# Folding the lift of the softmax exponent into the rows of the maxima

## The reference

```python
q, k, v = (split_heads(ln(x) @ W.T) for W in (Wq, Wk, Wv))   # 4 x 16 heads, 1024 x 64
sim = einsum('bhid,bhjd->bhij', q, k) * DIM_HEAD ** -0.5
m = max(sim, axis=-1)
e = exp(sim - m)
attn = e / (sum(e, axis=-1) + 1e-10)
x = x + (attn @ v) @ Wo.T + bo
gate, y = fp4_linear(ln(x), w_gate), fp4_linear(ln(x), w_up)
x = x + fp4_linear(silu(gate) * y, w_down)
```

## Time and profile before

| | us |
|---|---|
| median of 3 runs | 1754.72 |
| the profiled execution | 1756.87 |
| its span in the trace | 1755.0 |
| PE busy | 1539.2 (88%) |
| DVE busy | 1435.4 (82%) |
| POOL busy | 1242.6 (71%) |
| ACT busy | 1218.8 (69%) |

### The profile page before, as it was taken

How to read it: one execution, slowest core, us unless ns; L and a number is a source line. 1 busy time by engine, 2 the same in 40 slices (tenths; PEclk the granted TensorE clock), 3 DMA queues, 4 the chain that set the end, 5 groups by cost and what they waited for, 6 DMA issues and landing times.

```text
span 1755.0 us, 35325 instructions
## 1 busy us (share of the span) xinstructions
PE 1539.2 (88%) x13828; PEld 1041.4 (59%) x13828; DVE 1435.4 (82%) x2441; ACT 1218.8 (69%) x2222; POOL 1242.6 (71%) x1369
## 2 busy tenths in 40 slices
PE   4798899999889988898988898888898888898966
PEld 2465566666666656565656665655665656666654
DVE  7778877777788888888888888888888888888767
ACT  3587778888667776677777677767676776677633
POOL 3587778888677777677776777767777777777753
PEclk7899999999999999999999999999999999999987
DMA  4000000000000000000000000000000000000000
GB/s 122 13 13 13 7 14 14 13 14 14 7 15 15 13 15 9 9 15 15 14 15 9 9 15 15 13 9 15 9 15 15 13 9 9 15 15 13 3 4 12
DMA packets 26372, 26.20 MB, mean 15 GB/s; under 512 B 4768, under 2 KB 18016, under 8 KB 26208
## 3 DMA queue, kind: packets, MB, share of 16 engines
q1 hardware_dynamic: 26208, 23.95, 5.7%
HBM read 4.80 MB, written 2.10 MB: 4 GB/s over the span
## 4 chain that ended last, share of the span: by engine, by line
DVE 43%; PE 40%; ACT 10%; POOL 4%; issue 3%; DMA 0%; DVEq 0%; ACTq 0%; POOLq 0%
DVE negm L818 13%; PE ob L548 11%; PE sm L502 7%; PE st L522 6%; PE st L520 6%; ACT probs L635 5%; DVE q_hl L766 4%; ACT k_hh L599 3%; DVE qv L982 3%; DVE qv L970 3%; DVE k_l L772 3%; DVE qv L980 3%; POOL p_low L386 2%; PE mb L463 2%; DVE q_small L966 2%
## 5 line engine op out<-in xcount | busy, mean ns | idle before, releaser
L386 POOL TENSOR_TENSOR p_low<-probs 128x512 f16<-128x512 f32 x1024 | 1086.9, 1072 | 403.8 <-ACT probs L635 402.5
L635 ACT ACTIVATE probs<-st,lift,exp_scale 128x512 f32<-128x512 f32 x1024 | 792.8, 778 | 302.2 <-PE st L522 278.3
L818 DVE TENSOR_REDUCE negm<-sm 128x1 f32<-128x1024 f32 x512 | 624.4, 1220 | 126.6 <-PE sm L502 121.2
L502 PE MATMUL sm<-k_hh,q_hl 128*128 128x512 f16 x1024 | 314.8, 390 | 122.6 <-DVE negm L818 119.7
L522 PE MATMUL st<-q_hm,k_l 66*128 66x512 f16 x1024 | 396.6, 387 | 0.0
L520 PE MATMUL st<-q_hl,k_hh 128*128 128x512 f16 x1024 | 394.5, 385 | 0.6 <-ACT probs L635 0.6
L548 PEld LDWEIGHTS ob<-v,probs 128*128 128x128 bf16 x4096 | 283.4, 99 | 128.3 <-issue 11.5
L548 PEld LDWEIGHTS ob<-v,p_low 128*128 128x128 f16 x4096 | 278.9, 98 | 124.9 <-issue 2.7
L548 PE MATMUL ob<-v,probs 128*128 128x129 f16 x4096 | 325.1, 222 | 0.1
L548 PE MATMUL ob<-v,p_low 128*128 128x129 f16 x4096 | 320.8, 221 | 2.0 <-POOL p_low L386 2.0
L649 ACT ACTIVATE oscl<-ob,rden 128x128 f32<-128x128 f32 x512 | 158.6, 364 | 53.9 <-DVE rden L808 53.8
(11 more groups left out here) (157 smaller groups left out, 1616.1 us busy)
## 6 DMA issues: line engine op xcount, KB each, us to landing
k_hh<-k_hh SPq DMA_DIRECT2D x64, 128.0 KB, 2.3
q_hm<-q_hl SPq DMA_DIRECT2D x64, 128.0 KB, 2.3
x<-x SPq DMA_DIRECT2D x4, 512.0 KB, 7.2
q_hm<-m_high SPq DMA_DIRECT2D x128, 1.0 KB
q_hm<-m_low SPq DMA_DIRECT2D x128, 1.0 KB
out<-x SPq DMA_DIRECT2D x24, 64.0 KB, 1.5
probs<-wq SPq DMA_DIRECT2D x1, 512.0 KB, 5.7
probs<-wk SPq DMA_DIRECT2D x1, 512.0 KB, 6.9
```

The costliest lines, as they stand in the source:

```text
L386: return pool.tensor_tensor(p_low[b][:, j, :], p, p.bitcast(BF16)[:, 1::2], ALU.subtract)
L502: pe.matmul(sm[:, s % 2, :], q_hl[n][:, t * P:(t + 1) * P], k_hh[n][:, (s % 2) * 512:(s % 2 + 1) * 512], start=True, stop=True).then_inc(s ...
L635: nc.scalar.activation(probs[k % 2][:, s, :], st[s % 2][:, :], ACT.Exp, bias=lift[:, 0:1], scale=exp_scale[:, head, pair:pair + 1]).then_i ...
L818: nc.vector.tensor_reduce(negm[k % 2][:, s // 2:s // 2 + 1], sm[:, :, :].rearrange("p a n -> p (a n)"), AX.X, ALU.max, negate=True).then_i ...
```

## The change

The lift is no longer added by the exponential, which now has no bias operand. It is added to the rows of the maxima: for each head the tile `lift` holds 64/1024 divided by the head's top scale (at most 2**14), so that the scale of the exponential turns it into 8 again. The job `m` therefore multiplies `negm` by a diagonal of 1/1024 with a matmul in place of the transpose, ACT adds the head's lift with the function Identity and a bias operand, and DVE adds it as a scalar operand. Where the cap of 2**14 holds, the lift is smaller, so the constant beside the sums is made for each head too: `eps_lifted` comes from the setup through one exponential, one more small DVE operation follows at the start of round 1, and L805 takes it as a scalar operand. The setup makes `ident_unit` on POOL and has three more DVE operations and one more activation.

```diff
--- before.py
+++ after.py
@@ -35,7 +35,7 @@
 LIFT = 64.0
 MAX_UNIT = 1024.0
 TINY = 2.0 ** -126
-EPS_LIFTED = SM_EPS * math.exp(SCALE * LIFT)
+LIFT_TOP = 2.0 ** 14
 VC = 2 * DH + 1
 OT = 256
 
@@ -164,7 +164,9 @@
         exp_scale = sb("exp_scale", [P, 2, PAIRS])
         k_inv = sb("k_inv", [P, PAIRS])
         k_scale = sb("k_scale", [P, PAIRS])
-        lift = sb("lift", [P, 1])
+        lift = sb("lift", [P, 2, PAIRS])
+        eps_lifted = sb("eps_lifted", [P, 2, PAIRS])
+        ident_unit = sb("ident_unit", [P, P])
         w_inv = sb("w_inv", [P, 3, PAIRS])
         wT = [sb(f"wT_{part}", [P, 3, PAIRS, P], F16) for part in ("high", "low")]
         wo_s = sb("wo_s", [P, PAIRS, DIM])
@@ -200,6 +202,7 @@
         s_ws = [sem(f"{w}_scaled") for w in ("wq", "wk", "wv", "wo")]
         s_ks = sem("head_scale_step")
         s_kt = sem("head_scale_turned")
+        s_le = sem("eps_lifted_made")
         s_wt = sem("w_turned")
         s_wh = sem("wT_high_made")
         s_we = sem("wT_low_made")
@@ -236,6 +239,11 @@
         ffn = Ffn(nc, sb, sem, st, sm_banks, ob, mb, probs, p_low, xn,
                   (stats, mv, var_eps, rstd), (eps, half))
 
+        def lift_of(g, unit):
+
+            pair = (g - 1 + unit // 4) % PAIRS
+            return lift[0:IT, unit // 2 % 2, pair:pair + 1]
+
         def output_of(g, q, k, bank):
 
             back = 1 if bank == 0 else 2
@@ -333,6 +341,10 @@
             pool.wait_ge(s_id, 1)
             pool.affine_select(out=ident[:, :], in_=ident[:, :], compare_op=ALU.not_equal, fill=1.0,
                                base=0, pattern=[[-1, P]], channel_multiplier=1).then_inc(s_id, 1)
+            pool.memset(ident_unit[:, :], 0.0).then_inc(s_id, 1)
+            pool.wait_ge(s_id, 3)
+            pool.affine_select(out=ident_unit[:, :], in_=ident_unit[:, :], compare_op=ALU.not_equal, fill=1.0 / MAX_UNIT,
+                               base=0, pattern=[[-1, P]], channel_multiplier=1).then_inc(s_id, 1)
             ffn.constants(pool)
             pool.wait_ge(s_hf, 2)
 
@@ -473,14 +485,15 @@
 
                     unit = JOBS[n][ON_PE][0]
                     wait(pe, s_mx, 4 * (4 * (g - 1) + unit + 2))
-                    last = pe.transpose(bank[0:IT, 0:P], negm[(unit + 1) % 2][:, :], ident[:, :])
+                    last = pe.matmul(bank[0:IT, 0:P], negm[(unit + 1) % 2][:, :], ident_unit[:, :], start=True, stop=True)
                 last.then_inc(mb_ready[JOBS[n][1]], 1)
 
             def round_(g, r, q):
                 prev, cur, nxt, ffn_x, ffn_h = flags(r)
                 if r == 1:
 
-                    pe.wait_ge(s_init, 8)
+                    pe.wait_ge(s_init, 7)
+                    pe.wait_ge(s_id, 4)
                     pe.wait_ge(s_ws[3], 1)
                 for k in range(4):
                     head, half = k // 2, k % 2
@@ -582,6 +595,9 @@
                 nc.scalar.activation(wT[0][:, n // 2, n % 2 * 4:n % 2 * 4 + 4, :].rearrange("p a n -> p (a n)"),
                                      ([a[:, :] for a in st + ob] + sm_banks)[n], ACT.Copy).then_inc(s_wh, 1)
 
+            act.wait_ge(s_ks, 11)
+            nc.scalar.activation(eps_lifted[:, :, :], eps_lifted[:, :, :], ACT.Exp, scale=MAX_UNIT).then_inc(s_le, 1)
+
             def take(name, g, r, q, m):
                 bank, c = mb[JOBS[m][1]], int(name[1:] or 0)
                 cols = slice(c * HALF, (c + 1) * HALF)
@@ -593,7 +609,7 @@
                                              ).then_inc(s_hi, 1)
                 elif name[0] == "k":
                     if g == 0:
-                        act.wait_ge(s_ks, 8)
+                        act.wait_ge(s_ks, 11)
                     wait(act, mb_ready[JOBS[m][1]], ready)
                     for h in range(2):
                         nc.scalar.activation(k_hh[2 * (1 - q) + h][0:DH, cols], bank[h * DH:(h + 1) * DH, :], ACT.Copy,
@@ -616,8 +632,8 @@
                     ffn.take_scalar(name, bank)
                 elif name[0] == "m":
                     wait(act, mb_ready[JOBS[m][1]], ready)
-                    nc.scalar.activation(m_high[(JOBS[m][ON_PE][0] + 1) % 2][:, :], bank[0:IT, 0:P],
-                                         ACT.Copy, scale=1.0 / MAX_UNIT).then_inc(s_mh, 1)
+                    u = JOBS[m][ON_PE][0] + 1
+                    nc.scalar.activation(m_high[u % 2][:, :], bank[0:IT, 0:P], ACT.Identity, bias=lift_of(g, u)).then_inc(s_mh, 1)
 
             def round_(g, r, q):
                 prev, cur, nxt, ffn_x, ffn_h = flags(r)
@@ -632,7 +648,7 @@
 
                                 wait(act, s_pv, 2 * (unit - 1))
                             pair, head = (g - 1) % PAIRS, k // 2
-                            nc.scalar.activation(probs[k % 2][:, s, :], st[s % 2][:, :], ACT.Exp, bias=lift[:, 0:1],
+                            nc.scalar.activation(probs[k % 2][:, s, :], st[s % 2][:, :], ACT.Exp,
                                                  scale=exp_scale[:, head, pair:pair + 1]).then_inc(s_ex, 1)
                         if s == 2 and (prev if k < 2 else cur):
                             scaled(g, q, k, 1)
@@ -693,7 +709,6 @@
             def ones(n):
                 nc.vector.memset(k_l1[n][DH:DH + 2, :], MAX_UNIT).then_inc(s_init, 1)
 
-            nc.vector.memset(lift[:, :], SCALE * LIFT).then_inc(s_init, 1)
             nc.vector.memset(ones_8[:, :], 1.0).then_inc(s_init, 1)
             for n in range(3):
                 ones(n)
@@ -741,8 +756,14 @@
                 for h in range(2):
                     rows = slice(h * DH, (h + 1) * DH)
                     nc.vector.reciprocal(k_inv[rows, :], tops[rows, h, :]).then_inc(s_ks, 1)
+                nc.vector.reciprocal(lift[:, :, :], tops).then_inc(s_ks, 1)
                 dve.wait_ge(s_ks, 7)
                 nc.vector.tensor_tensor(k_scale[:, :], qk_scale[:, :], k_inv[:, :], ALU.mult).then_inc(s_ks, 1)
+                dve.wait_ge(s_ks, 8)
+                nc.vector.tensor_scalar(lift[:, :, :], lift[:, :, :], LIFT / MAX_UNIT, LIFT_TOP, ALU.mult, ALU.min
+                                        ).then_inc(s_ks, 1)
+                dve.wait_ge(s_ks, 10)
+                nc.vector.tensor_tensor(eps_lifted[:, :, :], lift[:, :, :], exp_scale[:, :, :], ALU.mult).then_inc(s_ks, 1)
 
             for n in range(6):
                 if n == 2:
@@ -776,8 +797,9 @@
                 elif name[0] == "m":
                     u, number = (JOBS[m][ON_PE][0] + 1) % 2, 4 * (g - 1) + JOBS[m][ON_PE][0] + 2
                     wait(dve, s_mh, number)
-                    nc.vector.scalar_tensor_tensor(out=m_low[u][:, :], in0=bank[0:IT, 0:P], scalar=1.0 / MAX_UNIT,
-                                                   in1=m_high[u][:, :], op0=ALU.mult, op1=ALU.subtract).then_inc(s_mr, 1)
+                    nc.vector.scalar_tensor_tensor(out=m_low[u][:, :], in0=bank[0:IT, 0:P],
+                                                   scalar=lift_of(g, JOBS[m][ON_PE][0] + 1), in1=m_high[u][:, :],
+                                                   op0=ALU.add, op1=ALU.subtract).then_inc(s_mr, 1)
                 elif name[0] == "v":
                     part = v[1 - q][:, 4 * c:4 * c + 4, :, :]
                     wait(dve, s_vh, 2 * g + c + 1)
@@ -798,17 +820,26 @@
                     wait(dve, s_x2, 2 * (g - 2) + c)
                     nc.vector.tensor_tensor(dst, dst, bank[:, :], ALU.add).then_inc(s_x2, 1)
 
+            def eps_unlift():
+
+                dve.wait_ge(s_le, 1)
+                nc.vector.tensor_scalar(eps_lifted[:, :, :], eps_lifted[:, :, :], SM_EPS, None, ALU.mult).then_inc(s_le, 1)
+                dve.wait_ge(s_le, 2)
+
             def sums(g, q, k, bank):
 
-                at = output_of(g, q, k, bank)[0]
+                at, _, head, _ = output_of(g, q, k, bank)
                 wait(dve, s_pv, at + 1)
-                nc.vector.tensor_scalar(den[:, bank, :], ob[bank][:, 2 * DH:2 * DH + OT + 1:OT], EPS_LIFTED, None, ALU.add
-                                        ).then_inc(s_nr, 1)
+                pair = (at // 2 // 4) % PAIRS
+                nc.vector.tensor_scalar(den[:, bank, :], ob[bank][:, 2 * DH:2 * DH + OT + 1:OT],
+                                        eps_lifted[:, head, pair:pair + 1], None, ALU.add).then_inc(s_nr, 1)
                 wait(dve, s_nr, 2 * at + 1)
                 nc.vector.reciprocal(rden[:, bank, :], den[:, bank, :]).then_inc(s_nr, 1)
 
             def round_(g, r, q):
                 prev, cur, nxt, ffn_x, ffn_h = flags(r)
+                if r == 1:
+                    eps_unlift()
                 for k in range(4):
                     unit = 4 * (g - 1) + k
                     for s in range(SLOTS):
```

## The result

The changed kernel takes 1762.38 us (median of 6 runs, 1760.24 to 1764.94) against 1754.76 for the kernel before, a ratio of 1.0045 with a 95% interval of 1.0032 to 1.0058: +7.6 us. The profiled execution took 1763.81 us with a span of 1761.7. The prediction was +4.8 us.

What follows compares the result with a forecast made beforehand. No engine fills the span, so the chain of waits was taken to decide. Its raw sum of +5.2 us, corrected by -3.6, +2.2 and +1.0, gave +4.8 us: 1759.5 us predicted, range 1749 to 1768.

Steps and rivals of the forecast that it cites:

- rival 5: Exponential on ACT keeps its 778 ns because an absent bias is fetched like a given one: +12.6 us, 1767.3; chance 0.05.
- The term of `den`: Scalar operand of `den` (L805) on DVE costs 0.06 us on 82 pieces of the chain: +4.9 us.
- rival 2: It cancels: `den` on DVE hides its scalar fetch in the overlap; -0.1 us, 1754.6; chance 0.23.
- The terms of `m_high` and `m_low`: Added operands on the chain: `m_high` on ACT 53 x 0.09 = +4.8 us, `m_low` on DVE 49 x 0.06 = +2.9 us.
- correction (a): Once in each of 24 feed-forward rounds DVE's L966 waits for POOL, so 0.15 us in front costs nothing: -3.6 us.
- rival 1: In feed-forward rounds POOL's `p_low` hides DVE and ACT terms, exponentials keep their gain: -4.3 us, 1750.4; chance 0.18.
- (b): PE's job `k1` waits for `m_low` in 31 rounds, losing 0.07 us of the gain in each: +2.2 us.
- (c): Three small DVE operations in the setup and one at the start of round 1: +1.0 us, between 0.4 and 2.5.
- The term of the exponential: Exponential (L635) on ACT loses 90 ns without its bias; 111 pieces on the chain give -10.0 us.
- The term of the matmul: Matmul replacing transpose L476 adds one PE instruction of 0.12 us; 22 pieces on the chain give +2.6 us.
- Rival 4: Matmul on PE takes four times the transpose, 22 x 0.2 = 4.4 us more: +9.2 us, 1763.9; chance 0.04.
- rival 3: PE becomes the bound; all 128 second instructions count, the exponential's gain nowhere: +18.3 us, 1773; chance 0.07.

Runs made afterwards that it cites:

- e2: Kernel before with the lift left out: exponential without bias operand, constant beside the sums 1e-10 itself; 1735.09 us.
- e5: Kernel before with only the operands of job `m` as in the change: `m_high` by Identity with zero bias, `m_low` with its scalar from a tile; 1756.76 us.
- e1: Kernel before with only the matmul against a diagonal of 1/1024 in place of the transpose, no 1/1024 on ACT and DVE; 1716.15 us.
- e3: Kernel before with only the constant of `den` read as a scalar operand from a tile in place of an immediate; 1760.61 us.
- e8: Kernel before with the matmul in place of the transpose plus zero bias and scalar operands in job `m`, exponential and `den` unchanged; 1750.73 us.
- e12: Kernel before with the matmul in place of the transpose, each such matmul issued twice (four instructions in place of two); 1733.64 us.
- e9: Kernel before without the quantiser's small step that POOL holds (L966), its factor moved into the following product as a scalar; 1702.56 us.
- e11: Changed kernel with the quantiser's held small step (L966) taken out, its factor moved into the following product; 1711.72 us.
- e7: Changed kernel with a bias operand of zeros given back to the exponential; 1759.59 us, its ten runs from 1746.9 to 1765.5.
- e10: Kernel before with the lift left out and the quantiser's held step (L966) removed, its factor moved into the following product; 1694.65 us.
- e6: Kernel before with the matmul in place of the transpose and the lift left out (exponential without bias); 1707.81 us.

## Why the prediction came out near, and what was wrong in it

The sign and the sum were right (+4.8 against +7.6, inside the range), and much of that was luck. Set side by side by stretch, with the forecast's terms shared out by its own counts, in us:

| | forecast | measured |
|---|---|---|
| to the end of round 4 | +1.9 | +5.2 |
| rounds 5 to 9 | +2.2 | +4.4 |
| rounds 10 to 31 | +0.8 | -4.3 |
| behind them | -0.1 | +1.3 |

e4, the changed kernel with the transpose, splits the sum in two, and in it, in the kernel before and in the changed one the step is held in every round with feed-forward. Everything but the matmul gives -8.9 us (1746.3 against 1755.3) where my terms had +2.2. The matmul on top of that gives +16.1 (1762.4 against 1746.3) where I had +2.6. Two errors of more than 10 us nearly cancelled. Nor do the parts add when each is put into the kernel before alone: the matmul gives -39, the missing bias -20, `den` +5.4, the operands of `m` -0.2 us, and together they give +7.6.

**The step that failed** is the one that the last paragraph suspected, that each piece of the chain keeps its place. In the rounds 10 to 31 the chain of before holds 88 pieces of the exponential and none of the transpose. Counted in the same way, the chain of the changed kernel holds there no exponential and 44 pieces of the matmul, 14.3 us. With the exponential quicker and the job `m` dearer, the longest path there runs through PE and DVE, so the exponential's gain arrived in part and the matmul's cost came in. The quicker exponential alone does not do this (e2 still has its 88 pieces); with the operands beside it 22 are left (e4).

**The prices of the operands** held. The exponential lost 93 ns (90 predicted), `m_low` gained 64 (60), `den` 61 (60). `m_high` gained 104 (90), and that is two things: in e5 the bias operand alone takes it from 254 to 346, 92 ns, and in e1 it takes 266 behind the matmul without any operand, 12 ns more. The Trainium skill, page "ScalarE: Activation LUTs", section "What ACT_TABLE_LOAD costs", gives 93 ns for each such operand of ACT, and the trace agrees with 93 and 92. The trace of the changed kernel has one table load, as before, so the rival of 328 us is out; the exponential's 685 ns put rival 5 out.

**The term of `den`**, 82 x 0.06 = +4.9, has the size that e3 measured, +5.4 us, and rival 2's zero is outside of e3's interval (3.0 to 7.0). But the place is another: 66 of the 82 pieces, 4.0 us, stood in the rounds with feed-forward, and e3's rounds 10 to 31 are only 0.05 us longer each, 1.1 in all. One more fall of the clock (13 against 12) gives 1.65, and 2.5 lie before round 5. Here too the sum agrees better than its parts.

**The terms of `m_high` and `m_low`** (+4.8 and +2.9, less 3.6 by correction (a)) came to nothing in e5: -0.2 us, though the interval of one thousandth leaves up to 1.8. Correction (a) took off 24 of the pairs only. POOL's hold of the small step is not the whole reason: in e8's nine rounds without it the operands cost 0.04 us (51.07 against 51.03 in e1), and in the plain rounds, where no such hold is in front, they cost nothing either (43.56 in both). What else hides them was not tested. With most of the `den` term missing in these rounds too, rival 1, by which DVE's and ACT's terms cost nothing there and the exponential keeps its gain, was nearer to e4 than my forecast.

**Corrections (b) and (c)** did not come. PE's wait for `m_low` at L447 was to grow from 11.1 us to some 13 to 19; in the changed kernel it is 0.9 us. The job `m` of (0,1) stands in front of that wait, and its longer matmul fills it. The setup's +1.0 is not to be seen: the first `m_high` starts at 50.03 us in place of 49.99, and round 2 at 97.44 in place of 97.64.

**The term of the exponential**, -10.0, is what e2 gives in its rounds without the fall of the clock: 22 x 0.44 = 9.7 us. What I had not seen is that it also makes six falls fewer, 6 x 1.65 = 9.9 us. Which waits bring a fall stays open: in the rounds 10 to 31 of before 12 of 22 equal waits do.

**The term of the matmul**, +2.6, was too low in its price everywhere and in its count in the rounds with feed-forward. The price: I took 0.12 us for a second instruction from eight f32 matmuls in a row, but the job `m` stands alone between f16 matmuls, and the pauses on either side cost another 0.18: 0.11 became 0.41. In the plain rounds the count held. Three of the four jobs lie on the chain before and after, 3 x 0.30 = 0.90, and e1 measures 0.93; the fourth is the one that fills PE's wait. In the rounds with feed-forward I counted two in all, none of them in the rounds 10 to 31, and there e4 shows 0.21 us a round (52.05 against 51.84), 4.6 in all, and three falls of the clock more (11 against 8), another 5. Rival 4 (the Trainium skill, page "TensorE: Matmul & The Clock Gate", section "Terms": the transpose mode is four times faster for FP32) put 4 x 0.11 = 0.44 on the job, near the 0.41 measured, and its 1763.9 us is nearer to the result than my forecast. That is not by its rule: in e12 one more f32 matmul adds 0.22, twice the transpose, and the rest of the 0.41 is the pauses. In the plain rounds the bound was PE, as in rival 3; it cost 3.9 us over the four of them. Rival 3's 18.3 us for all 128 jobs did not come.

**The last paragraph's warning** named what mattered most, and I gave it no price: DVE's steps that wait for POOL change with the phase, and "a different phase could move the time by more than the whole sum". By e8 the phase of 0.16 us in one short chain is worth 35 us (1716.2 to 1750.7), by e9 the step with its hold and the falls of the clock behind it 54 us. The Trainium skill, page "SBUF — State Buffer", section "SBUF: two separate sides", states why so little decides: DVE and GpSimd share a pair of ports by an exclusive lock, and whichever of a two-port DVE operation and a GpSimd operation starts first keeps it for its whole length. The trace agrees for DVE: the held step of before ends 0.03 to 0.04 us behind the end of `p_low` each time. For POOL it shows less than the rule says: behind the step of 0.18 us `p_low` takes 1.08 in place of 1.04.

**What the change itself costs**, with the hold out of the way, is e11 against e9: +9.2 us by the medians, 7.3 by the spans of the profiled executions (1707.9 and 1700.6). Of these 7.3 the plain rounds give 4 x 0.98 = 3.9 and round 4 another 3.3; the rounds 10 to 31 gain 22 x 0.21 = 4.6, where ACT's saving does arrive; the rest, 4.7, lies in rounds 2, 3 and 9 (2.9) and the end. Round 4's part was not tested apart, but the runs point at a wait of PE for a quantised weight that it turns. It is 2.05 us long in the changed kernel, 2.05 in e4 and 2.18 in e11, in all three the clock falls at its end or within 1.1 us, and round 4 takes 50.6, 49.9 and 49.3 us. In e7, with the change's costs and a slower exponential, this wait is 1.31 us, the clock stays up, and round 4 takes 48.1, against 47.3 before. So most of the 3.3 us is no price of an instruction, but again a wait that grew and the clock behind it.

The fastest version is e10: 1694.65 us, 3.5% below the kernel before, with the lift left out and the quantiser's factor moved. With the lift kept, e9 gives 1702.56.

## What to carry to other kernels

Before adding up pieces of a chain, look for instructions of one kind and shape with two durations (0.18 and 0.97 us for 22 numbers): here another engine held them, and a change anywhere in front of them can be worth more than all its own terms. Take such a hold out first, then measure the change. Price a matmul in the surroundings in which it will stand: here an f32 one alone between f16 ones cost 0.41 us where the transpose of the same tile cost 0.11. And where two engines' paths are nearly as long as each other, a saving on one of them moves the chain to the other, so that terms counted at nothing on the old chain come in; look at the chain of the changed kernel even when the sum agrees.

## What the runs showed of the hardware that was not expected

- A DVE `tensor_scalar` of 128 x 22 f32 on SBUF takes 0.18 us in a pause of POOL and 1.07 when POOL's `tensor_tensor` started 0.01 us ahead.
- After PE had stood 2.1 us its clock fell in 12 of the rounds 10 to 31 of the kernel before, 6 of e2, 13 of e5, from the higher to the lower of its two levels, in the kernel before 0.6 to 1.5 us after it had started again, at a cost of 1.65 us; in the kernels without such a wait (e1, e6, e9 to e12) it fell in none of these 22 rounds.
- An f32 matmul of 4 stationary columns and 128 moving ones, two instructions in the trace, takes PE 0.41 us between f16 matmuls against 0.11 for the transpose; a second one right behind adds 0.22 in the timeline.
- A RECIPROCAL of 128 x 22 f32 on SBUF took 0.29 us in every execution of all kernels here, also while POOL's `p_low` ran.
